# A fused vision-and-text layer on one core: a re-written order of the first stage, first loads on semaphores of their own, and a ring of four for the experts' outputs

## The reference, cut to what matters

```
x (64 images), txt (64 x 128 x 192)
h  = concat(tokens(layernorm(patches(x)) @ W + b + pos), txt)     # 64 x 324 x 192
h  = h + mamba(layernorm(h))          # per image, channel d of 192, state n of 16, along t of 324:
     s[t] = exp(delta[t] * A[n]) * s[t-1] + delta[t] * B[t,n] * u[t];   y[t] += C[t,n] * s[t]
h  = h + moe(layernorm(h)):
     shared = (silu(z @ Wsg) * (z @ Wsu)) @ Wsd                    # 192 -> 928 -> 192, every token
     routed : sigmoid gate, top 6 of 128 experts, the first 192 tokens of each expert are kept,
              silu(z @ Wg_e) * (z @ Wu_e) @ Wd_e   (192 -> 464 -> 192), times the gate, added back
```

## Time and profile before

| what | value |
|---|---|
| median of 3 runs | 4759.75 us (4747.87 to 4792.27) |
| the profiled execution | 4760.37 us, its span 4758.6 us |
| mean granted TensorE clock | 0.939 |
| busy share: PE, DVE, POOL, ACT | 83%, 72%, 63%, 55% |
| DMA traffic | 473.54 MB, 99 GB/s over the span |

### The profile page before, as it was taken

How to read it: one execution, slowest core, us unless ns; L and a number is a source line. 1 busy time by engine, 2 the same in 40 slices (tenths; PEclk the granted TensorE clock), 3 DMA queues, 4 the chain that set the end, 5 groups by cost and what they waited for, 6 DMA issues and landing times. The chain is left out here.

```text
span 4758.6 us, 74520 instructions
## 1 busy us (share of the span) xinstructions
PE 3971.8 (83%) x22114; PEld 2963.9 (62%) x22114; DVE 3441.9 (72%) x5523; ACT 2596.9 (55%) x4807; POOL 2997.6 (63%) x1609
## 2 busy tenths in 40 slices
PE   4458888888888888888888888887887899899987
PEld 3345556655555565655566565555556788788877
DVE  1888888888787888878788888888516565566554
ACT  1467766766677666767766677766632222222221
POOL 0877777767676777767777777777404555555555
PEclk8579999999999999999999999999998999999999
DMA  3322323322232233222323332322107777777775
GB/s 84 78 74 69 91 70 82 89 79 75 70 88 72 70 84 87 78 75 70 91 70 84 93 77 70 91 60 74 41 14 182 177 177 177 173 184 181 180 171 127
DMA packets 243533, 473.54 MB, mean 100 GB/s; under 512 B 39644, under 2 KB 162080, under 8 KB 243220
## 3 DMA queue, kind: packets, MB, share of 16 engines
q1 hardware_dynamic: 203792, 429.90, 34.0%
q0 software_dynamic: 36864, 37.98, 5.3%
q10 hardware_dynamic: 2564, 1.82, 0.2%
HBM read 404.99 MB, written 64.56 MB: 99 GB/s over the span
## 5 line engine op out<-in xcount | busy, mean ns | idle before, releaser
L506 POOL TENSOR_TENSOR y<-y,state 128x972 f32<-128x972 f32 x448 | 1017.1, 2270 | 731.9 <-DVE state L667 730.7
L661 DVE TENSOR_TENSOR_SCAN ps<-ps,state 128x972 f32<-128x972 f32 x512 | 1115.2, 2183 | 131.8 <-ACT ps L529 100.6
L485 POOL TENSOR_TENSOR state<-du,b_rows 128x972 f32<-128x972 f32 x512 | 1164.1, 2290 | 10.4 <-POOL delta L496 7.1
L529 ACT ACTIVATE ps<-delta,a_neg 128x324 f32<-128x324 f32 x1536 | 732.9, 524 | 311.3 <-DVE state L667 281.0
L1039 POOL DMA_INDIRECT out_rows<-yo,scatter_idx x256 | 369.5, 1443 | 458.7 <-DMA out_rows<-yo,scatter_idx 266.9
L667 DVE TENSOR_TENSOR state<-ps,c_rows 128x972 f32<-128x972 f32 x512 | 591.0, 1164 | 22.2 <-DVE ps L661 0.5
L781 PE MATMUL ps<-ws_d,inter 116*98 116x192 f32 (+1 forms) x3072 | 549.0, 333 | 63.3 <-DVE inter L753 24.6
L781 PEld LDWEIGHTS ps<-ws_d,inter 116*98 116x98 f32 (+1 forms) x3072 | 503.4, 176 | 93.4 <-issue 32.7
L753 DVE TENSOR_TENSOR inter<-ag,ps 116x648 f32<-116x648 f32 x256 | 211.5, 826 | 447.3 <-PE ps L766 447.3
L763 PE MATMUL ps<-x2f,ws_g 128*116 128x324 f32 x1024 | 366.4, 484 | 170.7 <-DVE inter L753 165.9
L1170 PE MATMUL e_ps<-w_down,e_inter 116*96 116x192 f32 x2048 | 394.7, 351 | 98.9 <-DVE yo L1120 98.6
(11 more groups left out here) (172 smaller groups left out, 7554.5 us busy)
## 6 DMA issues: line engine op xcount, KB each, us to landing
c_rows<-bc_rows SPq DMA_DIRECT2D x256, 324.0 KB, 4.8
b_rows<-bc_rows SPq DMA_DIRECT2D x256, 324.0 KB, 5.6
w_lo<-in_we_up SPq DMA_DIRECT2D x128, 348.0 KB
w_down<-in_we_down SPq DMA_DIRECT2D x128, 348.0 KB
x_in<-in_x SPq DMA_DIRECT2D x32, 1176.0 KB, 8.7
w_hi<-in_we_up SPq DMA_DIRECT2D x256, 116.0 KB
image_cnt<-running_counts SPq DMA_DIRECT2D x256, 81.0 KB
w_lo<-in_we_up SPq DMA_DIRECT2D x128, 116.0 KB
```

Of the source, the lines that this page charges most:

```text
L485: nc.gpsimd.tensor_tensor(b.state[n % 4][:], b.du[t.p][:], row, ALU.mult).then_inc(input_ready, 1)
L506: nc.gpsimd.tensor_tensor(y, y, b.state[n % 4][:], ALU.add).then_inc(y_added, 1)
L529: ins = nc.scalar.activation(to[:, c * L:c * L + L], b.delta[t.p][:, c, :], ACT.Exp, scale=b.a_neg[:, c, k:k + 1])
L661: nc.vector.tensor_tensor_scan(s, s, b.state[k % 4][:].rearrange("p a t -> p (a t)"), 0.0, ALU.mult, ALU.add).then_inc(scan_done, 1)
```

## The change

It has five parts.

1. `ORDER`, all five lists of the first stage, is written anew. The set of pieces of a body is the same but for the body in which a few are counted: `decay` 0 and `fill_b` 0 move from the end of the list (for the next pair) to the start of the next body's list, the `emb_stats` of ACT likewise, and the `warm` that stood between the two `count` now stands at the end of the PE list.
2. In the second body (-1) alone, the embedding pieces of pair 1 are put behind everything else in every queue.
3. In `prepare`, the raw token weights lie in `h2[0]` in place of `x_in` (which is then not zeroed there), so SP can load the first images behind its small weights, on the semaphore `x_loaded`; behind them it issues the seven loads of `ws_g`, `ws_u` and `ws_d` on a semaphore `ws_loaded`. The waits on `loaded` cover 44 small loads. `up_g` on PE waits for `ws_loaded`.
4. In the second stage POOL's list is (`token` at lag -3, `scatter` at lag 2) in place of (`scatter` at lag 2, `token` at lag -4).
5. `yo`, `scatter_idx` and the semaphores `added` are rings of four in place of two.

```diff
 "pe":
-  (down_a 0)(down 0)(down_a 1)(resid 0)(down 1)(resid 1)(down_a 2)(down 2)
-  (up_g 0)(resid 2)(up_u 0)(count 0)(warm)(count 1)(emb_a 0)(up_g 1)
-  (emb 0)(up_u 1)(warm)(warm)(x2_turn 0)(up_g 2)(emb_a 1)(up_u 2)(emb 1)
-  (x2_turn 1)(up_g 3)(x2_turn 2)(up_u 3)(warm)(up_g 4)(x1_turn 0)(x1_turn 1)
-  (up_u 4)(warm)(x1_turn 2)(bc_values)(up_g 5)(gate 0)(gate 1)(up_u 5)
-  (warm)(step 0)(step 1)(up_g 6)(warm)(step 2)(up_u 6)(up_g 7)(warm)(up_u 7)
+  (down_a 0)(down 0)(resid 0)(down_a 1)(down 1)(resid 1)(down_a 2)(down 2)
+  (up_g 0)(resid 2)(up_u 0)(emb_a 0)(count 0)(up_g 1)(count 1)(emb 0)(up_u 1)
+  (warm)(up_g 2)(x2_turn 0)(emb_a 1)(up_u 2)(warm)(emb 1)
+  (x2_turn 1)(up_g 3)(x2_turn 2)(up_u 3)(warm)(x1_turn 0)(up_g 4)(x1_turn 1)
+  (x1_turn 2)(up_u 4)(bc_values)(up_g 5)(gate 0)(warm)(gate 1)(step 0)
+  (up_u 5)(step 1)(up_g 6)(warm)(step 2)(up_u 6)(warm)(up_g 7)(warm)(up_u 7)(warm)
 "dve":
-  (choose)(scan 0)(scan 1)(fill_c 0)(fill_c 1)(scan 2)(weigh 0)(fill_c 2)(scan 3)(fill_c 3)(scan 4)(weigh 1)(fill_c 4)
-  (scan 5)(ln2_stats)(up_u 0)(emb_scale)(fill_c 5)(scan 6)(ln2_apply)(up_u 1)(ln1_stats)(fill_c 6)(ln1_apply)
-  (scan 7)(fill_c 7)(scan 8)(up_u 2)(fill_c 8)(scan 9)(up_u 3)(fill_c 9)(scan 10)(fill_c 10)(up_u 4)(scan 11)
-  (emb_stats)(scan 12)(fill_c 11)(fill_c 12)(up_u 5)(scan 13)(fill_c 13)(scan 14)(fill_c 14)(up_u 6)(scan 15)(fill_c 15)(up_u 7)
+  (choose)(scan 0)(fill_c 0)(scan 1)(fill_c 1)(scan 2)(weigh 0)(fill_c 2)(scan 3)(scan 4)(fill_c 3)(weigh 1)(fill_c 4)(up_u 0)
+  (ln2_stats)(scan 5)(ln2_apply)(emb_scale)(fill_c 5)(up_u 1)(ln1_stats)(scan 6)(ln1_apply)(fill_c 6)
+  (scan 7)(fill_c 7)(up_u 2)(scan 8)(fill_c 8)(scan 9)(up_u 3)(fill_c 9)(scan 10)(fill_c 10)(up_u 4)(scan 11)(fill_c 11)
+  (scan 12)(fill_c 12)(scan 13)(fill_c 13)(up_u 5)(scan 14)(fill_c 14)(up_u 6)(emb_stats)(scan 15)(fill_c 15)(up_u 7)
 "act": (the places that the text below uses)
-  (up_g 0)(to_exp)(resid 2)(decay 5) ... (up_g 5)(gate 0)(to_exp)(gate 1)(decay 13)(step 0)(decay 14)(step 1)(up_g 6)
+  (up_g 0)(decay 5)(resid 2)(decay 6)(to_exp) ... (up_g 5)(gate 0)(decay 13)(gate 1)(to_exp)(step 0)(decay 14)(decay 15)(step 1)(up_g 6)
...
+    todo = [...]
+    return sorted(todo, key=lambda x: x[1] == -2 and x[0][:3] == "emb") if i == FIRST_BODY + 1 else todo
...
+                sp.dma_start(b.x_in[:], a["x"][0:2].rearrange("b p c t -> p b c t")).then_inc(x_loaded, 16)
+                for to, source in late:
+                    sp.dma_start(to, source).then_inc(ws_loaded, 16)
...
                     elif kind == "up_g":
+                        pe.wait_ge(ws_loaded, 16 * 7)
...
-    "pool": (("scatter", 2), ("token", -4)),
+    "pool": (("token", -3), ("scatter", 2)),
...
-    yo = ring(2, "yo", [HALF, 2, D])
+    yo = ring(RING, "yo", [HALF, 2, D])
-                        wait(pool, added[before.p], 32 * before.pair_uses() + 32)
+                        wait(pool, added[before.q], 32 * before.h + 32)
-                        wait(dve, added[t.p], 32 * t.pair_uses())
+                        wait(dve, added[t.q], 32 * t.h)
```

More of the change, by code:

```diff
@@ L62 @@
     "pe": (
[L63 to L66, removed]
@@ L67 @@
-        ("up_u", 2, 4), ("warm", 2, 4), ("x1_turn", -1, 2), ("bc_values", -1, 0), ("up_g", 2, 5), ("gate", 1, 0), ("gate", 1, 1), ("up_u", 2, 5),
-        ("warm", 2, 5), ("step", -1, 0), ("step", -1, 1), ("up_g", 2, 6), ("warm", 2, 6), ("step", -1, 2), ("up_u", 2, 6), ("up_g", 2, 7), ("warm", 2, 7),
-        ("up_u", 2, 7)
+        ("down_a", 3, 0), ("down", 3, 0), ("resid", 1, 0), ("down_a", 3, 1), ("down", 3, 1), ("resid", 1, 1), ("down_a", 3, 2), ("down", 3, 2),
+        ("up_g", 2, 0), ("resid", 1, 2), ("up_u", 2, 0), ("emb_a", -2, 0), ("count", 2, 0), ("up_g", 2, 1), ("count", 2, 1), ("emb", -2, 0), ("up_u", 2, 1),
@@ new lines @@
+        ("warm", 2, 1), ("up_g", 2, 2), ("x2_turn", 1, 0), ("find", 2, 0), ("emb_a", -2, 1), ("up_u", 2, 2), ("warm", 2, 2), ("emb", -2, 1),
+        ("x2_turn", 1, 1), ("up_g", 2, 3), ("x2_turn", 1, 2), ("up_u", 2, 3), ("warm", 2, 3), ("x1_turn", -1, 0), ("up_g", 2, 4), ("x1_turn", -1, 1),
+        ("x1_turn", -1, 2), ("up_u", 2, 4), ("bc_values", -1, 0), ("up_g", 2, 5), ("gate", 1, 0), ("warm", 2, 4), ("gate", 1, 1), ("step", -1, 0),
+        ("up_u", 2, 5), ("step", -1, 1), ("up_g", 2, 6), ("warm", 2, 5), ("step", -1, 2), ("up_u", 2, 6), ("warm", 2, 6), ("up_g", 2, 7), ("warm", 2, 7),
@@ L70 @@
+        ("up_u", 2, 7), ("warm", 1, 0)
     ),
     "act": (
-        ("down", 3, 0), ("decay", 0, 1), ("decay", 0, 2), ("resid", 1, 0), ("down", 3, 1), ("decay", 0, 3), ("decay", 0, 4), ("resid", 1, 1), ("down", 3, 2),
-        ("up_g", 2, 0), ("to_exp", 2, 0), ("resid", 1, 2), ("decay", 0, 5), ("count", 2, 0), ("emb_a", -2, 0), ("count", 2, 1), ("ln2_stats", 1, 0),
-        ("decay", 0, 6), ("up_g", 2, 1), ("emb_a", -2, 1), ("to_exp", 2, 1), ("ln2_apply", 1, 0), ("decay", 0, 7), ("ln1_stats", -1, 0), ("emb", -2, 0),
@@ L75 @@
[L75 to L78, removed]
@@ new lines @@
+        ("ln2_apply", 1, 0), ("decay", 0, 7), ("ln1_stats", -1, 0), ("up_g", 2, 2), ("to_exp", 2, 2), ("x2_turn", 1, 0), ("ln1_apply", -1, 0),
+        ("decay", 0, 8), ("decay", 0, 9), ("x2_turn", 1, 1), ("up_g", 2, 3), ("x2_turn", 1, 2), ("emb", -2, 1), ("to_exp", 2, 3), ("decay", 0, 10),
+        ("x1_turn", -1, 0), ("up_g", 2, 4), ("x1_turn", -1, 1), ("to_exp", 2, 4), ("x1_turn", -1, 2), ("decay", 0, 11), ("decay", 0, 12),
+        ("bc_values", -1, 0), ("up_g", 2, 5), ("gate", 1, 0), ("decay", 0, 13), ("gate", 1, 1), ("to_exp", 2, 5), ("step", -1, 0), ("decay", 0, 14),
@@ L80 @@
+        ("decay", 0, 15), ("step", -1, 1), ("up_g", 2, 6), ("to_exp", 2, 6), ("step", -1, 2), ("softplus", -1, 0), ("up_g", 2, 7), ("to_exp", 2, 7)
     ),
     "dve": (
-        ("choose", 2, 0), ("choose", 2, 1), ("choose", 2, 2), ("scan", 0, 0), ("scan", 0, 1), ("fill_c", 0, 0), ("fill_c", 0, 1), ("scan", 0, 2),
-        ("weigh", 2, 0), ("fill_c", 0, 2), ("scan", 0, 3), ("fill_c", 0, 3), ("scan", 0, 4), ("weigh", 2, 1), ("find_a", 2, 0), ("fill_c", 0, 4),
-        ("scan", 0, 5), ("ln2_stats", 1, 0), ("up_u", 2, 0), ("emb_scale", -1, 0), ("find", 2, 0), ("fill_c", 0, 5), ("scan", 0, 6), ("ln2_apply", 1, 0),
@@ L85 @@
[L85 to L88, removed]
+        ("choose", 2, 0), ("choose", 2, 1), ("choose", 2, 2), ("scan", 0, 0), ("fill_c", 0, 0), ("scan", 0, 1), ("fill_c", 0, 1), ("scan", 0, 2),
@@ L101 @@
+        ("load_c", -1, 0)
     ),
```

63 lines of the change are left out of this document (35 added, 28 removed).

## The result

The changed kernel takes 4382.7 us (median of three, 4370.4 to 4389.1) where the kernel before takes 4759.75: a ratio of 0.919, 95% interval 0.911 to 0.927. The profiled execution took 4370.4 us, its span is 4368.7, so 390 us lie between the two profiles.

A forecast was written before the change was run, and what follows sets the result against it. The prediction held that the fit of the five lists, with 15.2 us of PE waits per body, bounds the first stage and scatters the second. 4760.4 - 174 (order) - 12 (head) = 4574, forecast as 4575 us, range 4455 to 4735.

The forecast's parts named there:

- the order's term: First stage's new lists: fewer PE waits, 6.0 us per body, 174 us over 29 bodies, between 67 and 225.
- the rival of a slower clock: PE in the first stage: clock falls to 0.85, 148 us lost, 4908 us; chance 0.08.
- The 17 us allowed for a late ACT: First stage: more work ahead of silu 6 in ACT's list, estimated at 1.8 us per body, 17 in the window.
- the rows named as gone: PE's waits at `bc_values` (12.8), `step` (10.4), `count` (8.6) and `down_a` (6.5 us in the window), expected to vanish.
- the 79.6 of the sum: DVE's work per body in the first stage: 85.6 - 6.0 = 79.6 us, so DVE can follow at 97.9.
- the DVE step of 6.0 us: `ln1_apply`'s three tiny steps beside POOL's products: 6.0 us should go, within `up_g`'s wait for `inter`, 49.7 to 4.
- The tables: ACT's table loads: none counted; rival with two more on the path, 2.6 us per body, 4649 us; chance 0.14.
- three signs of being wrong: Steps still at 2 us, DVE's decay waits above 3 us per body, or scatter spacing moved by more than 0.4.
- The head: Preparation's earlier loads and the reordered body -1: 12 us won, between 3 and 20.
- The second stage: POOL's list gives nothing and rings of four zero, within 50 us either way; scatters set the pace.
- The rival of crowded scatters: Second stage: weight loads meet every scatter, 128 x 1.2 = 154 us back, 4728 us; chance 0.07.
- The lock: DVE's wait for POOL moves to `emb_stats`: the 6.0 us come back, the order gives nothing, 4748 us; chance 0.10.

The follow-up runs named there:

- pe_rows_back: The changed kernel with `bc_values`, `step` 1 and `count` 1 right behind their old neighbours in PE's list: 4651.9 us, ratio 0.976 to the kernel before.
- decays_behind: The changed kernel with decays 5, 6 and 13 behind `to_exp` in ACT's list: 4532.8 us, ratio 0.950 to the kernel before.
- order_only: The kernel before with the five new lists of the first stage and nothing else: 4365.1 us, ratio 0.912.
- rest_only: The changed kernel with the five old lists of the first stage, all other parts kept: 4778.6 us, ratio 1.000 to the kernel before.
- weigh_early: The changed kernel with the old second stage and `weigh` 1 ahead of `fill_c` 3 in DVE's list: 4339.3 us, ratio 0.911 to the kernel before.
- up_u2_late: The changed kernel with `up_u` 2 behind `scan` 8 in DVE's list, as before: 4464.0 us, ratio 0.935 to the kernel before.
- lock_back_fill: The changed kernel with `ln1_apply` behind `fill_c` 6 again and two more `warm` ahead of `x2_turn` 1: 4500.9 us, ratio 0.943 to the kernel before.
- before_warm: The kernel before with two more `warm` right ahead of `up_g` 3 in PE's list: 4793.4 us, ratio 1.005.

## Why the prediction was wrong

**The step that failed** is the size of the order's term, 6.0 us per body, and in it this sentence: "PE's work per body is the same, eight `warm` included; what can change is the 15.2 us of waits." The products are the same; their time is not. It fell by 3.6 us per body. Most of that is the clock: PE falls to the lower of its two levels behind many waits, and the new order has few such waits. The clock records of the two traces have 48 stretches at the lower level in the 29 bodies before, 233.6 us together, and 10 after, 56.8 us. PE was busy in them for 7.0 and 1.6 us per body; at half the clock that is an estimated 3.5 and 0.8 us lost, a difference of 2.7. The other 0.9 of the 3.6 no run explains. I had seen the case, four products in 2.51 us behind 3.90 of idle time, and used it only as the rival of a slower clock. pe_rows_back shows the price of such waits: rows booked at 3.3 us cost 9.5, 5.6 of it in PE's busy time.

**The waits themselves** fell by 9.0 and not 6.0. Three terms make up the difference of 3.0. The 17 us allowed for a late ACT, 1.8 per body, did not come: PE waits for silu 12.5 / 10.95 = 1.1 us per body, 11.9 / 9.6 = 1.2 before, and decays_behind shows that the moved decays save DVE 3.3. The second wait at `gate` came (8.0 and 7.0), but the two are 1.4 per body, not 2.0: 0.6. The row of `x` that I left out went from 0.7 to 0.1: 0.6. So 12.6 = 6.0 forecast + 3.0 of waits + 3.6 of PE's busy time; times 29 that is 174 + 87 + 104 = 365.

**What held.** The direction, and the mechanism of the waits: of the rows named as gone, those of `bc_values`, `step` and `down_a` are, and `count` has 2.2 us left of 8.6; the steps of `ln1_apply` are at 0.17. That DVE's work is the 79.6 of the sum is partly luck. The two layer norms give 5.2 us per body where 6.0 were booked, the embedding's steps 1.9 and `weigh` 0 1.8 that were not booked, and `weigh` 1 takes 2.9 back (means over the 29 bodies of both traces). That the DVE step of 6.0 us sits inside PE's row of 49.7 was too tame a reading: put back, 4.5 us of DVE's work cost 6.2 of body. The tables: one load more per body than before, and no cost of it to be seen in PE's wait for silu. The Trainium skill, ScalarE: Activation LUTs, What ACT_TABLE_LOAD costs, prices a switch at 2.66 us, drain included. The rows here have 1.283 each, and taking two away saved nothing.

None of the three signs of being wrong that the prediction named came: the steps are not at 2 us, DVE's waits for decays fell, and the scatters' spacing moved by 0.06. It had no sign for a gain larger than the forecast.

**The head.** 12 forecast for the loads and body -1. The third `delta` is 19.8 us earlier, 8.8 of that by the order (283.9 in order_only), 11.0 by these. The second profile of the changed kernel has it at 267.1, which makes 16.8, and rest_only gains 6.7; so the 12 is confirmed only roughly. In the whole time none of it shows (order_only and stage2_old, both 4365.1).

**The second stage.** Zero forecast within 50, 15 to 20 lost; the reading of the earlier trace rows, that `yo` was never the late one, holds for all 128 scatters. The rival of crowded scatters had the direction at a tenth of its 1.2 us per scatter.

**The other rivals.** The lock did not move to `emb_stats` but in part to `weigh` 1, where taking it away gives 0.4 us per body (weigh_early). The slower clock came the other way round, 0.96 to 0.99.

## What to carry to other kernels

A wait on PE is priced at its length only if the products behind it run at full speed; look at those products in the timeline before you sum, and read PE's busy time per turn as something that an order can change. Where lists wait for each other, a late step costs anything from little (1.9 us of DVE's work in weigh_early, 0.4 of body) to more than its length (2.2 us in up_u2_late, 3.3), so try the one exchange that puts it beside free work first. Such prices do not add: four pieces put back one by one cost 3.3, 5.2, 6.2 and 9.5 us per body, 24.2 together, and the whole change gained 12.6. Dummy products paid here where they stood in a wait with their bank free (lock_back_fill), and not where they had to wait for the bank themselves (before_warm).
